# Cross-attention and a routed feed-forward on one core: VectorE divides and normalises first, chooses experts a step later, ranks in another bank

## Time and profile before

| | |
|---|---|
| median of 3 runs | 215.69 us (215.64 to 215.78) |
| the profiled execution | 215.48 us |
| its span, first to last instruction | 213.7 us |
| attention steps 0 to 16 | about 33 to 109 us of the span |
| expert tiles | from 111.5 us of the span |
| mean granted TensorE clock | 0.994 of full speed |

### The profile page before, as it was taken

The page is one execution under the profiler, slowest core; times in us unless marked ns, Lnnn a source line. Parts: engine busy times, 40 slices in busy tenths (PEclk is TensorE's granted clock), DMA queues, the critical chain, the costliest instruction groups (busy, mean ns, idle before and its releaser), DMA issues.

```text
span 213.7 us, 5788 instructions
## 1 busy us (share of the span) xinstructions
PE 201.5 (94%) x1606; PEld 162.8 (76%) x1606; DVE 147.7 (69%) x523; ACT 142.3 (67%) x399; POOL 128.4 (60%) x230
## 2 busy tenths in 40 slices
PE   8999998999999999999979899999999999999972
PEld 2676575576766676676648789999999999998971
DVE  0269979877889969899977997534444344467583
ACT  2355896999886888678746757576666767666110
POOL 5226657023342588677767867888888887567120
PEclk9999999999999999999999999999999999999997
DMA  5997999999993001000024823232222222261394
GB/s 151 380 391 208 366 408 406 404 398 344 312 349 92 14 28 37 25 28 26 28 70 122 234 64 96 69 87 76 66 77 72 60 64 62 66 225 33 87 354 155
DMA packets 23601, 34.91 MB, mean 163 GB/s; under 512 B 2561, under 2 KB 15878, under 8 KB 23442
## 3 DMA queue, kind: packets, MB, share of 16 engines
q1 hardware_dynamic: 20610, 29.27, 40.9%
q0 software_dynamic: 2240, 4.23, 6.3%
q10 hardware_dynamic: 720, 1.02, 1.6%
HBM read 15.85 MB, written 19.06 MB: 163 GB/s over the span
## 4 chain that ended last, share of the span: by engine, by line
PE 61%; DVE 18%; POOL 6%; issue 5%; ACT 5%; DMA 3%; POOLq 0%; SPq 0%; DVEq 0%; ACTq 0%
PE pt_ps L1365 10%; PE score_ps L1323 5%; PE pt_ps L1374 5%; PE score_ps L1325 5%; PE score_ps L1324 5%; PE score_ps L1178 4%; PE pt_ps L1118 4%; PE ps_a L1228 3%; PE pt_ps L1216 3%; PE score_ps L1128 3%; DVE less L829 2%; DMA kheads<-y_rows 2%; ACT probs L405 2%; PE ps_a L1334 2%; POOL y_rows L620 2%
## 5 line engine op out<-in xcount | busy, mean ns | idle before, releaser
L620 POOL DMA_INDIRECT y_rows<-vals,ids x38 | 37.7, 993 | 11.2 <-ACT vals L477 4.4
L405 ACT ACTIVATE probs<-score_ps,less 128x128 f32<-128x128 f32 x128 | 37.4, 405 | 1.7 <-DVE less L829 1.7
L597 POOL DMA_INDIRECT x_rows<-stage,slot x32 | 32.6, 1020 | 9.2 <-issue 7.7
L1365 PE MATMUL pt_ps<-w,probsT 128*128 x234 | 32.6, 275 | 0.9 <-DVE probsT L1018 0.6
L1365 PEld LDWEIGHTS pt_ps<-w,probsT 128*128 128x128 f32 x234 | 30.8, 190 | 1.6 <-issue 1.4
L477 ACT ACTIVATE vals<-pt_ps,xg 128x128 f32<-128x128 f32 x38 | 13.9, 367 | 26.6 <-PE pt_ps L1365 26.6
L1045 DVE TENSOR_TENSOR xg_low<-ps_a,xg_high 128x128 fp32r<-128x128 f32 x40 | 11.6, 290 | 28.8 <-ACT xg_high L459 28.4
L1323 PE MATMUL score_ps<-w_high,xg_low 128*128 x80 | 29.2, 365 | 0.0
L1325 PE MATMUL score_ps<-w_high,xg_high 128*128 x80 | 25.9, 323 | 0.0
L1324 PE MATMUL score_ps<-w_low,xg_high 128*128 x80 | 25.6, 320 | 0.0
L1053 DVE TENSOR_TENSOR probs<-probs,score_ps 128x352 f32<-128x352 f32 x40 | 20.8, 520 | 6.4 <-ACT probs L466 3.6
(11 more groups left out here) (179 smaller groups left out, 442.8 us busy)
## 6 DMA issues: line engine op xcount, KB each, us to landing
x_rows<-pads SPq DMA_DIRECT2D x1, 9945.0 KB, 37.2
w_low<-in_w13T SPq DMA_DIRECT2D x3, 1056.0 KB, 10.5
xg<-x_rows SPq DMA_DIRECT2D x40, 65.0 KB, 1.8
ctx_r<-in_ctxT SPq DMA_DIRECT2D x4, 512.0 KB, 7.1
y_rows<-pads SPq DMA_DIRECT2D x1, 2048.0 KB, 18.1
w<-in_w2T SPq DMA_DIRECT2D x1, 1728.0 KB, 12.6
kheads<-y_rows SPq DMA_DIRECT2D x3, 512.0 KB, 5.2
mask_b<-in_mask SPq DMA_DIRECT2D x4, 256.0 KB, 7.5
```

The source lines that it names most:

```text
L405: last = nc.scalar.activation(probs[:, r % 2, h, :], score_ps[:, r % 2, h, :], ACT.Exp, bias=less[:, r % 2, h:h + 1])
L597: pool.indirect_dma_start(x_rows[:, :], bass.IndirectOffsetOnAxis(ap=slot[:, par, c, p:p + 1], axis=0), stage[:, par, c, p, :], None, boun ...
L620: pool.indirect_dma_start(y_rows[:, :], bass.IndirectOffsetOnAxis(ap=ids[:, s:s + 1], axis=0), yt[:, s, :], None, bounds_check=last_row, o ...
L1365: last = nc.tensor.matmul(into[:, 0:D], hidT[:, q3, c, :], w2[:, bass.ds(e3, 1), c, :].rearrange("p o d -> p (o d)"), start=(c == 0), stop ...
```

## The change

On DVE, within a step:

- `unturn` is split into `inverse` and `divide`; these and `norm2` move ahead of both `maxima`.
- The choice of experts (`find_top` to `mark_both`) moves from step 4g+7, after `second`, to step 4g+8, between the second `maxima` and `second`. The keys stay at step 4g+7, but are spread between the division, `norm2` and the maxima.
- Weights, ranks and labels move from step 4g+8 to step 4g+9: `keep_ranks` first, then `weigh_and_label` between the two `maxima`, with instructions of weights and labels in turn. For group 2 this falls behind the last step.
- `low(8)` (a subtraction of 128x704, L693) moves from step 9 to step 10; `table_counts(0)` from step 13 to 14, `table_rows(0)` from step 14 to 16, `table_used(0)` and `table_counts(1)` from ahead of the tiles into tiles 0 to 2.

On PE: `rank(g)` moves from `turn_rows` of step 4g+8 to `turn_out` of step 4g+9 and writes into `ps_a`; the product with the values (L1228) then waits until `keep_ranks` has read them; the 18 fillers in `turn_rows` are gone; the first tile waits for the ranks of group 2.

```diff
-LOWS = {1: (0, 1, 2), 2: (3,), 3: (4,), 4: (5,), 5: (6,), 6: (7,), 9: (8,)}
+LOWS = {1: (0, 1, 2), 2: (3,), 3: (4,), 4: (5,), 5: (6,), 6: (7,), 10: (8,)}
...
+        def ranks_of(g):
+            return (ps_b, 3 * P + GZ) if g == NG - 1 else (ps_a, 2 * P)
+        def ranked_ahead_of(b):
+            return (b + 1) // UN - 2 if b % UN == UN - 1 and b >= 2 * UN - 1 else None
...
-                ins.then_inc(route_chain, 1)
-                dve.wait_ge(route_chain, g * sum(LINKS.values()) + before + route_links[stage_name])
+                ins.then_inc(route_chain, 1)
+                made[name] = route_links[0]
+            def known(name):
+                dve.wait_ge(route_chain, made[name])
...
+            def weigh_and_label(g):
+                pick_slots(g)
+                pick(g)
+                sum_slots(g)
+                sum_picked(g)
+                add_both(g)
+                invert_total(g)
+                store_weights(g)
+                label_rows(g)
...
             def step(k, r, i):
+                keyed, marked, labelled = routed(k, r, UN + 3), routed(k, r, 2 * UN), routed(k, r, 2 * UN + 1)
+                if labelled is not None:
+                    keep_ranks(labelled)
+                if on(k, 2):
+                    inverse(k - 2, r % 2)
+                    divide(k - 2, r % 2)
+                if keyed is not None:
+                    add_one(keyed)
+                if on(k, 3):
+                    norm2(k - 3)
+                if keyed is not None:
+                    invert(keyed)
                 if on(k, 0):
                     maxima(k, r, 0)
-                if on(k, 2):
-                    unturn(k - 2, r % 2)
-                if on(k, 3):
-                    norm2(k - 3)
+                if keyed is not None:
+                    over_knee(keyed)
+                if labelled is not None:
+                    weigh_and_label(labelled)
                 if on(k, 0):
                     maxima(k, r, 1)
+                if keyed is not None:
+                    stretch(keyed)
+                if marked is not None:
+                    find_top(marked)
+                    find_places(marked)
+                    mark_top(marked)
+                    mark_both(marked)
                 for expert in LOWS.get(k, ()):
                     low(expert)
-                if routed(k, r, UN + 3) is not None:
-                    make_keys(routed(k, r, UN + 3))
-                if routed(k, r, 2 * UN) is not None:
-                    weigh(routed(k, r, 2 * UN))
-                if k == 3 * UN + 1:
+                if k == 3 * UN + 2:
                     table_counts(0)
-                if k == 3 * UN + 2:
-                    table_rows(0)
                 if on(k, 2):
                     dve.wait_ge(o_mm, k - 1)
                     if routed(k, r, UN + 2) is not None:
                         logits_of(routed(k, r, UN + 2))
-                    if routed(k, r, 2 * UN) is not None:
-                        keep_ranks(routed(k, r, 2 * UN))
                     second(k - 2)
-                if routed(k, r, UN + 3) is not None:
-                    choose(routed(k, r, UN + 3))
-                if routed(k, r, 2 * UN) is not None:
-                    place_rows(routed(k, r, 2 * UN))
-                    label_rows(routed(k, r, 2 * UN))
+                if k == NB:
+                    table_rows(0)
                 if routed(k, r, UN + 2) is not None:
                     clamp(routed(k, r, UN + 2))
...
             turns(step)
-            unturn(NB - 1, 1)
+            keep_ranks(NG - 2)
+            inverse(NB - 1, 1)
+            divide(NB - 1, 1)
             norm2(NB - 2)
-            table_used(0)
-            table_counts(1)
+            weigh_and_label(NG - 2)
...
             def within(k):
+                if k == 0:
+                    table_used(0)
+                if k == 1:
+                    count_tiles(1)
+                if k == 2:
+                    pass_tiles(1)
...
                     pe.wait_ge(v_set, b + 1)
+                    if ranked_ahead_of(k - 2) is not None:
+                        pe.wait_ge(ranks_kept, ranked_ahead_of(k - 2) + 1)
...
                 pe.wait_ge(o_copied, b + 1)
+                if ranked_ahead_of(b) is not None:
+                    rank(ranked_ahead_of(b))
...
                 if on(k, 2):
-                    if k >= 2 * UN and k % UN == 0:
-                        keep_busy(2 * ((k - 1) % 2), 8 if k == 3 * UN else 5)
                     pe.wait_ge(normed, k - 1)
-                    if routed(k, k % UN, 2 * UN) is not None:
-                        rank(routed(k, k % UN, 2 * UN))
...
                     pe.wait_ge(ld_tile[r], i * 16 + 16)
+                    if k == 0:
+                        pe.wait_ge(ranks_kept, NG - 1)
```

More of the change, by code:

```diff
@@ L726, in _, with route_link @@
                     spread(j)
-            route_links = {}
-            LINKS = {"clamp": 1, "keys": 4, "choose": 3, "weigh": 4, "place": 2}
-            def route_link(g, stage_name, ins):
-                route_links[stage_name] = route_links.get(stage_name, 0) + 1
-                before = sum(n for name, n in LINKS.items() if list(LINKS).index(name) < list(LINKS).index(stage_name))
+            route_links, made = [0], {}
+            def route_link(name, ins):
+                route_links[0] += 1
@@ L761, in make_keys, with invert, over_knee @@
-            def make_keys(g):
-                add_one(g)
-                above_knee(g)
+                route_link("one_more", nc.vector.tensor_scalar(sigs[:], sigs[:], 1.0, None, ALU.add))
+            def invert(g):
+                known("one_more")
+                route_link("sigs", nc.vector.reciprocal(sigs[:], sigs[:]))
+            def over_knee(g):
+                known("sigs")
+                knee = sigs[:, GZ:GZ + 1]
+                route_link("over", nc.vector.tensor_scalar(over[:], sigs[:, 0:GZ], knee, knee, ALU.max, ALU.subtract))
@@ L766, in find_top, with stretch, find_places @@
+            def stretch(g):
+                known("over")
+                route_link("key", nc.vector.scalar_tensor_tensor(flat_key, over[:], STRETCH, flat_key, ALU.mult, ALU.add))
             def find_top(g):
-                route_links.clear()
+                known("key")
                 for b in range(UN):
                     last = nc.vector.max(top[:, b, :], key[:, b, :])
-                route_link(g, "choose", last)
+                route_link("top", last)
+            def find_places(g):
+                known("top")
@@ L781, in mark_top, with mark_both @@
-                assert route_links["choose"] == LINKS["choose"]
+                route_link("choices", last)
+            def mark_both(g):
+                known("choices")
                 if g >= 1:
@@ L794, in _, with pick, sum_picked, add_both @@
             flat_choices, flat_of, flat_slots = (t[:].rearrange("p c b e -> p c (b e)") for t in (choices, chosen_of, slots_of))
[L796 to L803 removed]
+            def pick(g):
+                known("choices")
+                route_link("picked", nc.vector.tensor_tensor(flat_of, flat_choices, of_choices(sigs[:, 0:GZ]), ALU.mult))
+            def sum_picked(g):
+                known("picked")
+                route_link("sel_sig", nc.vector.tensor_reduce(sel_sig[:], chosen_of[:], AX.X, ALU.add))
+            def add_both(g):
+                known("sel_sig")
+                route_link("total", nc.vector.scalar_tensor_tensor(total[:], sel_sig[:, 0, :], TOP_EPS, sel_sig[:, 1, :], ALU.add, ALU.add))
+            def invert_total(g):
+                known("total")
+                route_link("share", nc.vector.reciprocal(total[:], total[:]))
+            def store_weights(g):
+                known("share")
                 for p in range(UN):
```

83 lines of the change are left out of this document (40 added, 43 removed).

## The result

The changed kernel takes 222.8 us (median of four runs, 221.76 to 225.01); the kernel before took 215.66 beside it. The ratio is 1.036 (1.031 to 1.042). It is slower, as forecast, but by 7.1 us and not by 3.1, and outside the range. Its four runs differ by 3.2 us, and the slower ones have the lower mean granted clock: 0.980 and 0.979 in the two runs of 221.8, 0.966 in the one of 223.8, 0.956 in the one of 225.01. The last is the profiled execution; its span is 223.2 us, 9.5 above that of before.

The account below looks back on a forecast made before the run. Ordinary steps were taken as bound at 4.37 us by the PE-ACT-PE loop. Terms -2.64 + 0.1 + 4.3 + 0.4 + 1.2 = +3.3 on 215.48 gave 218.8 us, range 214.8 to 221.0.

Parts of the forecast that it names:

- steps 8, 12: With choice and fillers gone from there, both steps fall to the 4.37 of ACT's loop: -2.64 us.
- ranks, steps 9, 13: Rank products ahead of the output's turn on PE take 0.2 us: +0.1 for both steps.
- late label, steps 10, 14: POOL waits 2.4 us for the label, delaying root and norm2: +2.1 and +2.2 us, +4.3 in all.
- steps 11, 15: Step 11 loses its 0.1 excess, step 15 gains 0.5 from table_counts ahead of second: +0.4 us.
- label of group 2: Behind the steps, the later label delays scatter, block 15's root and norm2, shifting the tiles: +3.3 instead of +2.0.
- table late for SP: Tables moved into tiles 0 to 2 costed at nothing; table_rows(0) in step 16 given no loss of its own.
- clock: Granted clock 1.00 in all seven windows, taken as unchanged without the fillers: 0 us.
- The mechanism that decided the sign: Labels half a step later make POOL wait in its ordered list, so norm2 and steps 10 and 14 run late: +4.3.
- The first two rivals: First: quotient waits set the steps, 214.8 us, chance 0.15. Second: the label's lateness is absorbed, 215.2 us, chance 0.13.
- priced that as a rival: PE's waits in steps 10 and 14 without fillers lower the clock; one such step costs up to 4.4: 223.2, chance 0.10.
- Step 16 itself comes out even: In step 16, five fillers go while table_rows(0) comes ahead of the last division: no net change.
- Costing the earlier division at nothing: In ordinary steps ACT's two probability copies hold up L448, so an earlier quotient on DVE gains 0.

Follow-up runs that it names:

- e1: Changed kernel with nine filler products back in turn_rows of steps 10 and 14, ahead of the wait for norm2; 221.72 us, ratio 1.028.
- e5: Changed kernel with weights and labels of groups 0 and 1 right behind keep_ranks, ahead of division and norm2; 219.44 us, ratio 1.018.
- e2: Changed kernel with the first table's counts back in step 13 and its rows back in step 14; 219.20 us, ratio 1.020.
- e4: Kernel before with only division and norm2 moved ahead of both maxima; 217.35 us, ratio 1.011.
- e6: e5 with the first table back in steps 13 and 14 as in e2; 216.70 us, ratio 1.008.
- e9: e6 with the kernel before's order of maxima, division and norm2 in every step but 9 and 13; 216.23 us, ratio 1.005.
- e10: Changed kernel with DVE's routing and table work spread over its idle places, the table's rows in step 16 ahead of second; 215.29 us, ratio 1.000.
- e11: e10 with the table's rows right behind norm2 in step 16, ahead of the choice of group 2; 213.85 us, ratio 0.994.

## Why the prediction was wrong in size

The span grew by 9.5 us in the profiled execution. Held against the forecast's terms:

| term | forecast | measured | from |
|---|---|---|---|
| steps 8, 12 | -2.64 | -2.64 | table above |
| ranks, steps 9, 13 | +0.1 | +0.1 | table above |
| late label, steps 10, 14 | +4.3 | +4.45 | 2.28, and 2.17 in e1 at full clock |
| steps 11, 15 | +0.4 | +0.45 | e1, at full clock |
| label of group 2 | +1.2 | not seen | see below |
| table late for SP | 0 | +2.2 | 10.73 against 8.51 |
| clock | 0 | +4.8 | 1.36 in step 11, 0.83 in 14, 1.62 in 15 (against e1), 1.0 in the tiles |

With 0.1 ahead of step 8 the measured ones make 9.5. Of the clock's 4.8, filling the waits of the steps gave back 3.0 in e1's span: step 13 and the stretch to the first tile were 0.3 and 0.4 longer there. The mean clock of the other runs is higher, so less of the clock's term is in the median of 222.8. The two fastest, at 221.8, lie 3.0 above the forecast; their mean clock is that of e1's profiled execution (0.980), whose only low stretch ahead of the last slice is in the first tiles. So in them the steps probably kept the clock, which no trace of them shows, and the table and the first tiles are what the forecast missed.

The mechanism that decided the sign was right, and so were the sizes of the four terms in the steps: the label ready at 74.29 (forecast 74.1), step 11 at 80.55 (80.3), ordinary steps unchanged, the quotient's waits gone without a gain. In steps 11 and 15 the sum came nearer than its parts, by luck: +0.11 and +0.34 at full clock (e1), where -0.1 and +0.5 were forecast. The first two rivals fell with that.

The step that failed is the sentence on the clock, "I take it as unchanged". The forecast had PE waiting "2 us and more in steps 10 and 14" and priced that as a rival, with a chance of 0.10 and "PE still works on either side of each wait" against it. That did not hold: both waits were followed by the lower level, and so was the wait ahead of the first tile, which the rival had not named. And it was no rival: it comes on top of the late label, so its price had to stand in the upper end of the range, up to 221.0, and not beside it.

The second failed step is "Step 16 itself comes out even". It followed the moved table on DVE's list alone. Its reader is SP, whose first load comes 2.8 us or more behind the rows; in the kernel before the rows were made at 98.40 and the load came at 109.60, and that cover went with the move: 10.73 us from step 16 to the first tile in place of 8.51, and 10.97 and 11.17 in e5 and e1, which have the table in the same place.

The term for group 2's label named a wait that occurred (POOL's 2.76 at 118.05), but not its effect: POOL's root of block 15 was there by 123.26, and `norm2` of block 15 began at 124.12, behind tile 0's hidden product on the same engine (123.68, 0.52 long). In e2, without the low clock and the late table, `norm2` of block 15 stands 3.53 behind the first tile where it stood 3.13, and "rest" is 0.2 longer: in that execution the term is 0.2 to 0.4, not 1.2.

Costing the earlier division at nothing held for ordinary steps; alone, in e4, it costs 1.8 us in the steps with routing or table work, by DVE's chain. How much of that the changed kernel pays beside the label's wait was not tried alone; without that wait, on e6, the old order gains 0.7 in step 15 (e9).

## What to carry to other kernels

When an edit adds a wait in one piece to the matrix engine, cost the wait and, in the upper end of the range, the next stretch at the lower clock, which not every run has to pay, and try whether filler products in that wait bring the clock back. When small work is moved later, follow its readers on every queue, SP's register reads too, and not only the list it is moved on. And before moving work ahead of other work on one engine, write down what then stands between one result of the loop and the next: what had filled another engine's latency may land in the loop.

## What was not expected of the hardware

Single waits of PE of 2.20, 2.04 and 3.23 us in the changed kernel were each followed by a stretch at the lower level (0.72, 0.61 and 0.59 in the windows behind them); waits of 1.56 and 0.77 in step 14 of e2 were not, its step 15 ran in 5.04 at 1.00. The length of one wait does not decide it: ahead of the first tile, 1.43 in e6 was followed by a fall (0.66 over the first 4.98 us of tiles), 1.56 in e9 was not (1.00 over 5.78). The changed kernel's runs differed by 3.2 us, with mean clocks from 0.956 to 0.980, while the runs of the kernel before beside them lay within 0.3 us (within 1.7 in the widest of the later sets). And SP's first load came 2.8 to 3.0 us behind the end of DVE's instruction that makes the table's rows in the four kernels in which these were late (changed 2.79, e5 2.79, e10 2.92, e11 3.03).
